# Keys projected three units earlier, attention scores two units later, and two DMA queues in the prologue

## The reference

```python
x = x + attn_block(layernorm(x))     # below
x = x + ffn(layernorm(x))            # 128x128 weights quantised to int4, plus a low-rank term

# attn_block, with x the normalised input
xn = layernorm(x) * ln_g + ln_b
dt_in, Bs, Cs = split(xn @ w_xproj)                    # 64, 64, 64 columns
delta = softplus(dt_in @ w_dt + b_dt)
h_t = exp(delta_t * A) * h_(t-1) + (delta_t * xn_t) * B_t      # 128 channels x 64 states
y_t = sum over states of h_t * C_t ;  ssm = (y + x * D_ssm) @ w_ssm_out
q, k, v = x @ wq, x @ wk, x @ wv     # 16 heads of 8, 4 key/value heads
# local attention: blocks of 32 queries against 96 keys, with a relative bias and a mask
attn = softmax(q k^T / sqrt(8) + bias) v @ wo
conv = silu(causal 4-tap depthwise conv(x))
mem  = x @ w_wm + b_wm + 0.3 * softmax(x dec^T / sqrt(128)) dec    # 512 memory slots
return x + 0.2 * attn + 0.45 * ssm + 0.15 * conv + 0.2 * mem
```

## Time and profile before

| | |
|---|---|
| median of 3 runs | 1215.29 us (1210.8 to 1216.22) |
| the profiled execution | 1216.41 us |
| its span, first to last instruction | 1214.6 us |
| busy share: VectorE / PE / ACT / POOL | 88% / 73% / 67% / 67% |
| mean granted TensorE clock | 0.848 |

### The profile page before, as it was taken

The page is one execution under the profiler, slowest core; times in us unless marked ns, Lnnn a source line. Parts: engine busy times, 40 slices in busy tenths (PEclk is TensorE's granted clock), DMA queues, the critical chain, the costliest instruction groups (busy, mean ns, idle before and its releaser), DMA issues. The chain is left out here.

```text
span 1214.6 us, 19663 instructions
## 1 busy us (share of the span) xinstructions
PE 887.2 (73%) x4292; PEld 364.4 (30%) x4292; DVE 1071.7 (88%) x2434; ACT 810.5 (67%) x2199; POOL 816.0 (67%) x558
## 2 busy tenths in 40 slices
PE   4286788687777786787767687768777777687775
PEld 1122333333323232332323233233332323232232
DVE  3389999989988999899989999898998899889993
ACT  4277784777746776578746877477775778556772
POOL 6466775767766776667766777576776677657663
PEclk9558898879886888878878989787988888888987
DMA  4543455434553444534454345543555434554430
GB/s 115 126 132 122 130 136 148 131 102 142 139 152 109 123 134 132 164 114 115 133 138 141 114 135 135 147 131 104 143 139 151 124 119 135 140 139 133 126 116 9
DMA packets 124133, 155.38 MB, mean 128 GB/s; under 512 B 32722, under 2 KB 57062, under 8 KB 124006
## 3 DMA queue, kind: packets, MB, share of 16 engines
q1 hardware_dynamic: 123494, 153.74, 45.7%
q0 software_dynamic: 512, 0.27, 0.2%
HBM read 137.63 MB, written 4.52 MB: 117 GB/s over the span
## 5 line engine op out<-in xcount | busy, mean ns | idle before, releaser
L1343 POOL TENSOR_TENSOR prod<-hst,C 128x1024 f32<-128x1024 f32 x256 | 603.9, 2359 | 337.2 <-DVE hst L1155 337.2
L1155 DVE TENSOR_TENSOR_SCAN hst<-bank,dbx 128x512 f32<-128x512 f32 x512 | 620.6, 1213 | 2.5 <-ACT bank L630 2.5
L630 ACT ACTIVATE bank<-wide,A_rep 128x512 f32<-128x512 f32 x512 | 351.6, 687 | 292.5 <-DVE hst L1155 274.1
L1149 DVE TENSOR_TENSOR dbx<-bank,B 128x512 f32<-128x512 f32 x512 | 344.6, 673 | 76.3 <-PE bank L875 70.8
L875 PE MATMUL bank<-spread,sel_bc 96*128 96x512 bf16 x512 | 216.2, 434 | 58.8 <-DVE dbx L1149 45.2
L644 ACT ACTIVATE prob<-s_sb,nmax 128x96 f32<-128x96 f32 x512 | 183.9, 360 | 0.0
L906 PE MATMUL bank<-k,q 128*128 128x384 f32 x256 | 133.2, 607 | 58.8 <-DMA k<-uv 37.2
L896 PE MATMUL bank<-prod,sel_red 128*32 128x512 f32 x1024 | 161.8, 709 | 4.4 <-POOL prod L1343 4.4
L913 PE MATMUL bank<-ident,prob 128*96 128x128 f32 x512 | 89.0, 303 | 63.9 <-ACT ao L660 61.3
L875 PEld LDWEIGHTS bank<-spread,sel_bc 96*128 96x128 bf16 x512 | 55.0, 108 | 201.7 <-DVE dbx L1149 119.1
L1348 POOL TENSOR_TENSOR prob<-prob,pinv 128x384 f32<-128x384 f32 x128 | 106.4, 831 | 9.8 <-DVE pinv L1176 7.6
(11 more groups left out here) (180 smaller groups left out, 915.2 us busy)
## 6 DMA issues: line engine op xcount, KB each, us to landing
wide<-dt_rows SPq DMA_DIRECT2D x512, 256.0 KB, 4.3
vw<-v_tok SPq DMA_DIRECT2D x80, 64.0 KB, 3.7
spread<-parts SPq DMA_DIRECT2D x96, 32.0 KB, 3.5
x_sb<-in_L_attn_x_dram SPq DMA_DIRECT2D x8, 256.0 KB, 4.4
dt_rows<-sp_t SPq DMA_DIRECT2D x8, 256.0 KB, 4.4
out_dram<-outb SPq DMA_DIRECT2D x8, 256.0 KB, 2.3
q<-qn SPq DMA_DIRECT2D x112, 16.0 KB
vw<-v_tok SPq DMA_DIRECT2D x16, 48.0 KB, 3.6
```

The lines of the kernel that those rows point to most:

```text
L630: nc.scalar.activation(daP[s % 2][:, :], wide[m % SLOTS][:, s % 2, :], ACT.Exp, scale=A_rep[:, g:g + 1]).then_inc(exp_done, 1)
L1149: v.tensor_tensor(dbx[:, s % 3, :], uP[s % 2][:, :], B2[p][:, :], ALU.mult).then_inc(dbx_done, 1)
L1155: v.tensor_tensor_scan(hst[:, s % 4, :], daP[s % 2][:, :], dbx[:, s % 3, :], 0.0, ALU.mult, ALU.add).then_inc(scan_done, 1)
L1343: g.tensor_tensor(prod[:, 2 * (m % 4):2 * (m % 4) + 2, :], hst[:, 2 * (m % 2):2 * (m % 2) + 2, :], C2[p][:, :].unsqueeze(1).to_broadcast([ ...
```

## The change

Three tables are altered, one DMA function is made usable by other engines, and the prologue's issue order is altered.

- `JOB_AT`: k from slot 56 to 53, v from 62 to 63. `KEY_DMA_AT` stays 30.
- `SCORES_AT`: every block two slots later (2, 5, 8, 11, 15, 18, 21, 25, ... 51). All lags stay, so bias, exponentials, transposes, values and copies move by two slots too; block 15's values are now in slot 63.
- `VALUE_DMA_AT`: three DMAs each at m = 0 to 3 in place of two each at m = 0 to 5.
- Prologue on SP: high parts, `wide` pair 0, keys, `wide` pairs 1 to 3, weights, values. The middle and low parts' eight DMAs go to ScalarE's queue, behind its last job (the copy of v) and ahead of its first unit exponential.

```diff
-          48: ("m", "es3"), 51: ("p", "q"), 52: ("m", "pt2"), 55: ("m", "pt3"), 56: ("p", "k"),
-          62: ("p", "v")}
+          48: ("m", "es3"), 51: ("p", "q"), 52: ("m", "pt2"), 53: ("p", "k"), 55: ("m", "pt3"),
+          63: ("p", "v")}
-VALUE_DMA_AT = {0: (0, 0), 1: (0, 2), 2: (1, 0), 3: (1, 2), 4: (2, 0), 5: (2, 2)}
+VALUE_DMA_AT = {0: (0, 1, 2), 1: (3, 4, 5), 2: (6, 7, 8), 3: (9, 10, 11)}
-SCORES_AT = {33 * k // 10: k for k in range(NBLK)}
+SCORES_AT = {2 + 33 * k // 10: k for k in range(NBLK)}
+        def spread_parts(eng, B, p, part, c0):
+            wait(eng, sp_step, B * N_SP + SP[("hi", "mid", "lo")[part]])
+            for c in (c0, c0 + 1):
+                eng.dma_start(spread[p][32 * part:32 * part + 32, c, :],
+                             parts[32 * c:32 * c + 32, part, :]).then_inc(parts_in, 16)
-                        window_values(B, *VALUE_DMA_AT[m])
+                        window_values(B, VALUE_DMA_AT[m])
-                            spread_parts(B + 1, 1 - p, *PART_DMA_AT[m])
+                            spread_parts(sp, B + 1, 1 - p, *PART_DMA_AT[m])
-            def window_values(B, j, m0):
+            def window_values(B, which):
                 wait(sp, done["p"], job_count("p", B, "v"))
-                for m in (m0, m0 + 1):
+                for j, m in (divmod(n, 4) for n in which):
             def front(B, p):
                 store_rows(B, p)
-                for at in PART_DMA_AT.values():
-                    spread_parts(B, p, *at)
-                for m in range(SLOTS):
+                spread_parts(sp, B, p, 0, 0)
+                spread_parts(sp, B, p, 0, 2)
+                widen(B, p, 0)
+                keys(B)
+                for m in range(1, SLOTS):
                     widen(B, p, m)
-                keys(B)
                 load_weights()
                 for at in VALUE_DMA_AT.values():
-                    window_values(B, *at)
+                    window_values(B, at)
...
                     pre_job(name, B, p, front=True)
+                for part in (1, 2):
+                    spread_parts(act, B, p, part, 0)
+                    spread_parts(act, B, p, part, 2)
                 for s in range(AHEAD):
                     unit_exp(B, s)
```

More of the change, by code:

```diff
@@ L447, in load_weights @@
                 assert n == N_W_DMA
[L449 to L454, removed]
             def keys(B):
```

## The result

The changed kernel takes 1196.12 us (median of 4 runs, 1194.46 to 1197.29) against 1215.07 us for the kernel before on the same chip: ratio 0.9849, 95% interval 0.9823 to 0.9876. That is 19 us where 47 were forecast, and outside the range of 1148 to 1192. Its profiled execution took 1196.19 us, span 1194.4 us, mean granted clock 0.847.

What follows compares the result with a forecast made beforehand. VectorE paces the kernel, plus what TensorE is late. Gains of 17 (scores), 20 (values), 8 (other slots) and 10 (prologue) less 8 for coincidences make 47: 1169.4 us profiled, 1168 median, range 1148 to 1192.

Steps and rivals of the forecast that it cites:

- the 0.07 that the prediction left over: Remaining chance, 0.07, for a time between 1192 and 1210 us and about no change.
- The shift against jobs that stay: Slot 31 and single slots gain 8 us; scores and transposes meeting other work cost 8 us; the two cancel.
- the list of signs: What would show the forecast wrong, including waits over 1 us in slots 32, 36, 42, 49 or 52.
- Scores two slots later, 17 us: At batch starts, broadcasts go out before TensorE waits for keys: 17 us gained of 24.4 in seven batches.
- that rival: Batch start stays bound by TensorE at half clock, 2.9 us late in seven batches: 1181 us; chance 0.15, with variants 0.23.
- All waits vanishing: Rival: all alignment waits go and no new ones come, 1140 us; between that and 1158, chance 0.15.
- Values by threes, 20 us: Values land before their product, so the residual add's wait goes: 20 us gained of 20.4, lower bound 10.
- k, 0: Moving k from slot 56 to 53 does nothing by itself, since SP is late with the keys' DMAs: 0 us.
- My sign for it: Keys' DMAs starting earlier than 0.4 us after the batch's first product would show that k's move did matter.
- Prologue, 10 us: Batch 0: keys and query heads land earlier, and units 2 and 3 run in that wait; 10 us, range 5 to 12.
- The shared descriptor generator: Prologue: if SP's and ScalarE's DMA issues take turns, that part brings 5 us, not 10.
- The coincidences at half clock (slower): Rival: full slots 31, 35, 51, 41 and 48 run late at half clock, 90 us in eight batches: 1251 us; chance 0.03.

Runs made afterwards that it cites:

- scores back: The changed kernel with the scores at their places of before; 1189.1 us, ratio 0.9775 to the kernel before.
- after: The kernel before with the whole change made; 1196.12 us, ratio 0.9849.
- the best version: The changed kernel with scores one slot later than before instead of two and ffn two slots later; 1170.4 us, or 1168.1 with k in slot 56.
- threes alone: The kernel before with only the value transfers by threes; 1196.2 us, ratio 0.9827.
- k, v and threes: The kernel before with k in slot 53, v in slot 63 and value transfers by threes, scores and prologue unchanged; 1191.0 us, ratio 0.9822.
- k back: The changed kernel with k alone back in slot 56; 1196.8 us, ratio 0.9856 to the kernel before.
- prologue alone: The kernel before with only the new prologue issue order; 1212.3 us, ratio 0.9979.

## Why the prediction was wrong

The measured 1196 us lie between 1192 and 1210, in the 0.07 that the prediction left over and gave no mechanism.

- **The shift against jobs that stay: the step that failed.** I put the new coincidences at 8 us and the old waits that go in slot 31 and elsewhere at 8, "the two cancel". Against the kernel with scores back, the shift removes some 26 us there (15.0 in slot 31, 9.5 in 49 and 55, 1.7 in 21) and adds some 49 (23.3 in slots 22 and 23, 11.8 in slot 32, 10.9 in slots 17, 29 and 30, and 3 in slots 4 and 8). So a term put at nothing cost some 20. I had listed slots 31, 35, 41, 48 and 51, where pieces of TensorE's work meet, and weighed each by its sum of matmuls at full clock. Slot 32 was on the list of signs, with 1.4 us a batch; slot 22, the largest at 4, was not: its broadcast stands ahead of slot 21's scores and transposes in TensorE's list, so it isn't a meeting of pieces at all. What I left out is the chain ffn waits for (GpSimd's root, four normalisations, transposes, the copy fT behind probabilities and probT on ScalarE), the bias and maximum that had covered slot 21 and moved away, and the clock at half.
- **Scores two slots later, 17 us:** right in mechanism: the scores no longer wait for the keys, and slot 2's wait falls from 19.3 to 1.8, by 17.5. That this is my 17 is in part luck. 3.4 of it are batch 0's, and of the seven batches' 24.4 some 8 were already gone without the shift (15.9 left with the scores back). The start did stay at half clock, which I had argued against because TensorE fills such a stretch: in batch 4 the clock was 0.50 from 613.60 to 618.80 with TensorE busy for all of it. But unit 4's product waited 0.52 us and not the 2.9 of that rival. All waits vanishing is out as well.
- **Values by threes, 20 us:** 19.6 measured alone. The landing before the old slot 12 was enough; with it the shift adds nothing, though my working leaned on both, and without it the shift alone does the same.
- **k, 0:** 0.7 us in after and -2.3 in the best version, neither beyond its interval. The reason was half right. SP issues back to back, as I said, yet between threes alone and k, v and threes its keys come 1.3 us earlier against batch 4's first product (-1.00 and +0.30 us), where slot 55's new wait holds VectorE up and not SP. My sign for it (keys' DMAs earlier than 0.4 us behind the first product) was a bad one: they are 0.9 us ahead in batch 4 of after, but 1.6 ahead with k back.
- **Prologue, 10 us:** 2.2 alone (3.7 in the profiled executions). Issue times were right (36.87 and 38.96 where I had 37 and 38 to 39); unit 4 came at 50.85 where I had 48 to 50. Mis-sized is the landing: from their last issue to the first product there are 7.0 us (43.89 less 36.87), where before there were 2.6 (40.01 less 37.45). And the 10 held the units 2 and 3 that run while the scores wait, which is the shift's gain: of unit 4's 7.8 us the prologue alone has 3.3, and keeps them. The shift's part is mostly lost again up to the batch's end, slot 8's wait growing from 2.4 to 3.6 and slots 17 and 32 getting 1.0 and 2.8 in batch 0.
- **The shared descriptor generator.** The Trainium skill (Perfetto Trace Analysis, "DMA Instruction — HWDGE") says that such a DMA locks a generator that the issuing sequencers share. From that I had reckoned that issues would take turns, at twice 0.63 us each. The trace does not show this: seven of ScalarE's issues take 4.94 us, 0.71 each, and the keys' four that SP issues beside them take 2.79, exactly as before. A short lock would still fit the 0.71 against 0.63.
- **The coincidences at half clock (slower):** its mechanism is a part of what ate the gain, at half of its price and mostly at another place (slot 22; 1.7 of 3.1 us in batch 4). The 49 us of new waits come near the 54 (three fifths of its 90) from which it would have decided, and a chance of 0.03 was too small.

## What to carry to other kernels

When a stream of work is shifted against jobs that stay, list for each job not only what meets it on its own engine but the chain in front of it and what had covered its wait, and price it at the lower clock level too. Run such a shift by one, two and none, with the job that it meets moved as well: the gain here hung on the pair (20 us from ffn's move with one slot of shift, 0.6 with none). Of a change in several parts, time each alone: the transfers by threes alone gave as much as the whole, and two parts that each removed the same wait could not both be counted.

## What the runs showed of the hardware

ScalarE issued DMAs beside SP at 0.71 us each without slowing SP (2.79 us for four, as before). Transfers of 32 KB took 6.5 us to land in the median with two of 256 KB issued among them, and 4.0 with these two issued 2.7 us later; the first use came 1.2 us earlier. TensorE ran at half clock over stretches that it filled (3.40 of 3.40 us, and 5.20 of 5.20). And where the half clock falls can change several slots away from an edit: with ffn moved out of slot 21, a wait of 1.8 us in slot 29 went as well in each of batches 1 to 6, the half-clock stretch no longer lying over slot 28's scores.
